# One fused two-layer block: the first FFN's maximum by a TensorE transpose, its second product's bank waits, query tiles between the steps of head 0, and short products before waits

## What is computed

```python
x = x + tanh(g_xattn[0]) * _L0_xattn_ref(ctx, ctx, _layernorm(x), ssm_kernel, D, 8)
x = x + tanh(g_ffn[0])   * _L0_ffn_ref(_layernorm(x), w1, b1, w2, b2)
x = x + tanh(g_xattn[1]) * _L1_xattn_ref(_layernorm(x), ctx, ...)
x = x + tanh(g_ffn[1])   * _L1_ffn_ref(_layernorm(x), ...)
```

```python
def _quant_per_tensor(x):
    scale = jnp.maximum(jnp.max(jnp.abs(x)) / QMAX, EPS)
    q = jnp.clip(jnp.round(x / scale), -QMAX, QMAX).astype(jnp.int8)
    return (q, scale)
h = gelu(_dyn_quant_linear(hidden_state, w1, b1))   # quantises hidden_state
return _dyn_quant_linear(h, w2, b2)                 # quantises h: a second maximum
```

## Time and profile before

| | us |
|---|---|
| median of 3 runs | 646.97 |
| lowest, highest | 645.42, 648.0 |
| profiled execution | 647.98 |
| its span, first to last instruction | 646.1 |
| PE busy | 613.0 |
| DVE busy | 545.4 |
| ACT busy | 484.5 |
| POOL busy | 345.6 |

### The profile page before, as it was taken

The page is one execution under the profiler, slowest core; times in us unless marked ns, Lnnn a source line. Parts: engine busy times, 40 slices in busy tenths (PEclk is TensorE's granted clock), DMA queues, the critical chain, the costliest instruction groups (busy, mean ns, idle before and its releaser), DMA issues.

```text
span 646.1 us, 9452 instructions
## 1 busy us (share of the span) xinstructions
PE 613.0 (95%) x2831; PEld 361.9 (56%) x2861; DVE 545.4 (84%) x1063; ACT 484.5 (75%) x725; POOL 345.6 (53%) x430
## 2 busy tenths in 40 slices
PE   4899999999999899989999999999898999999997
PEld 4677777777777444544445565655433444444443
DVE  2597888889999788985779988889898999999865
ACT  4449786666754898999663567677679999999984
POOL 2479888888873175210001011113488989898861
PEclk9799999999999999999999999999999999999999
DMA  8949997699999364217628940000114666666661
GB/s 305 377 144 287 297 341 252 215 329 340 335 312 312 129 227 162 99 39 285 258 49 161 228 134 16 16 18 0 49 50 132 177 178 177 185 195 163 179 162 49
DMA packets 127860, 118.90 MB, mean 184 GB/s; under 512 B 83456, under 2 KB 90384, under 8 KB 126672
## 3 DMA queue, kind: packets, MB, share of 16 engines
q1 hardware_dynamic: 120384, 104.23, 52.7%
q10 hardware_dynamic: 7440, 14.24, 6.6%
HBM read 68.04 MB, written 30.49 MB: 153 GB/s over the span
## 4 chain that ended last, share of the span: by engine, by line
PE 65%; ACT 11%; DVE 11%; issue 7%; DMA 4%; POOL 1%; SPq 0%; DVEq 0%; ACTq 0%; POOLq 0%
PE ps L1184 22%; PE ps L1473 14%; PE ps L1489 8%; PE ps L1299 5%; ACT turn L970 4%; PE ps L1400 3%; PE ps L1430 3%; ACT arena L917 2%; PE ps L1448 2%; PE ps L1404 2%; PE ps L1193 1%; PE ps L1380 1%; PE ps L1390 1%; DVE turn L1857 1%; DMA arena<-kpad_d 1%
## 5 line engine op out<-in xcount | busy, mean ns | idle before, releaser
L1184 PE MATMUL ps<-arena 128*128 128x288 f32 x640 | 163.5, 413 | 6.2 <-DMA arena<-kpad_d 3.9
L1184 PEld LDWEIGHTS ps<-arena 128*128 128x128 f32 x640 | 121.1, 193 | 39.6 <-issue 4.5
L1473 PE MATMUL ps<-arena 128*128 128x512 bf16 x510 | 113.4, 379 | 3.6 <-DVE arena L2052 3.3
L1473 PEld LDWEIGHTS ps<-arena 128*128 128x128 bf16 x512 | 49.5, 98 | 65.5 <-DVE arena L2052 4.1
L683 POOL TENSOR_TENSOR arena<-arena 128x512 f32<-128x512 f32 x64 | 80.4, 1277 | 9.0 <-DVE arena L2052 8.3
L583 POOL TENSOR_TENSOR arena<-arena 128x1024 f32<-128x1024 f32 x32 | 60.6, 1895 | 22.5 <-issue 11.8
L1489 PE MATMUL ps<-arena 128*128 128x512 bf16 x241 | 57.1, 379 | 2.5 <-ACT arena L1084 0.7
L1299 PE MATMUL ps<-arena 128*128 128x512 bf16 (+1 forms) x248 | 56.2, 379 | 0.9 <-ACT arena L917 0.4
L1340 PE MATMUL ps<-arena 128*128 128x512 bf16 x251 | 55.3, 379 | 1.7 <-DVE arena L1827 1.4
L590 POOL TENSOR_TENSOR turn<-turn 128x512 f32<-128x512 f32 x31 | 40.5, 1308 | 21.6 <-DVE turn L1637 21.6
L2052 DVE SCALAR_TENSOR_TENSOR arena<-ps,up_scale,arena 128x512 f32<-128x512 f32 x64 | 46.6, 744 | 5.9 <-ACT arena L1060 5.0
(11 more groups left out here) (229 smaller groups left out, 1287.6 us busy)
## 6 DMA issues: line engine op xcount, KB each, us to landing
arena<-in_L_ffn_w SPq DMA_DIRECT2D x48, 512.0 KB, 6.0
arena<-kpad_d ACTq DMA_DIRECT2D x16, 512.0 KB, 6.9
hq_d<-arena SPq DMA_DIRECT2D x14, 512.0 KB, 3.1
tern_d<-late SPq DMA_DIRECT2D x24, 256.0 KB, 5.8
arena<-in_ctx SPq DMA_DIRECT2D x4, 1024.0 KB, 12.0
arena<-in_x SPq DMA_DIRECT2D x4, 1024.0 KB, 14.2
arena<-in_L_ffn_w ACTq DMA_DIRECT2D x8, 512.0 KB, 5.6
arena<-in_ctx SPq DMA_DIRECT2D x2, 2048.0 KB, 10.6
```

Source lines behind the costliest of these rows:

```text
L1184: last = pe.matmul(ps[:, 4 * s + lo, 0:NB * PAIRS], toep[:, u, (LB - 1 - lo + li) * P:(LB - lo + li) * P], kv[:, s, li, :], start=(li == 0 ...
L1473: last = pe.matmul(ps[:, bank, :], xq4T[:, s, 4 * j + k, :], w[:, k, c * L:(c + 1) * L], start=(k == 0), stop=(k == LB - 1))
```

## The change

- **Maximum.** PE transposes `am1`, spread over 128 columns, into bank 7 between theta 4 and theta 5; DVE reduces that bank (`amg`). POOL's first `partition_all_reduce` goes; the second stays.
- **Rows in halves.** DVE's two tiles of group 0 are counted on their own; PE turns them first, then ACT's two; DVE copies out in two pieces. All thresholds of `xqb_ready` and `xq_tr` rise by one.
- **Thetas.** On PE thetas 0 to 4 stand before the maximum, 5 before `rows_T(0)`, 6 and 7 behind it. On ACT copy 2 stands before `quant_x(0)`, 3 to 5 between it and `quant_x(1)`, 6 and 7 behind.
- **Fourth weight quarter** is cast by POOL after the second group's norm.
- **Second product.** PE waits for DVE's add out of the bank (`x2_added`). ACT's fourth piece has two tiles, DVE does tiles 14 and 15 after the cast of piece 1; SP's reload of the last x rows waits for that. 22 products of 128x128 before the wait for the weights take the place of ten of 128x512 behind it.
- **Opening.** `toep_load(0, 0)` after two copies; 40 identity transposes; query tiles after blocks 1 and 2; POOL's `pairs(1, 1)` waits for DVE's four normalised tiles.

The diff, cut:

```diff
                     sp.wait_ge(S["hq_ready"], 3)
+                if g == 3:
+                    sp.wait_ge(S["hq_ready"], 6)
...
             norm_x0(1)
+            pool.wait_ge(S["xn0_dve"], 4)
...
             norm_x1(1)
+            pool.wait_ge(S["o_done"], HEADS + 2)
+            pool.wait_ge(S["w1_in"], 16 * 4)
+            w = fw1T[:, :, 3 * L:4 * L]
+            pool.tensor_scalar(w, w.bitcast(I16), 1.0, 0.0, ALU.mult, ALU.add).then_inc(S["w1_ready"], 1)
...
-            pool.wait_ge(S["amax_ready"], 1)
-            pool.partition_all_reduce(amg[:, 0:1], am1[:, 0:1], P, RED.max).then_inc(S["amax_all"], 1)
...
             pool.wait_ge(S["xn1_ready"], NT)
-            pool.wait_ge(S["xqb_ready"], 2)
+            pool.wait_ge(S["xqb_ready"], 3)
...
                 pool.tensor_tensor(x_res[:, t, :], x_res[:, t, :], b2b[:, :], ALU.add).then_inc(S["xb_added"], 1)
-            pool.wait_ge(S["xqb_ready"], NG)
+            pool.wait_ge(S["xqb_ready"], NG + 1)
...
                 pool.tensor_tensor(x_res[:, t, :], x_res[:, t, :], b2b[:, :], ALU.add).then_inc(S["xb_added"], 1)
-            pool.wait_ge(S["xq_tr"], NG)
+            pool.wait_ge(S["xq_tr"], NG + 1)
...
             act.dma_start(kpad_d, kpad[:, :]).then_inc(S["k_stored"], 16)
-            for n in range(G):
+            for n in range(2):
...
             toep_load(0, 0)
-            for n in range(G, 2 * G):
+            for n in range(2, 2 * G):
...
                 normalise_x1(n)
-            for b in range(2, G + 1):
-                theta_out(b)
+            theta_out(2)
...
                 if g >= 2:
-                    act.wait_ge(S["xqb_ready"], g - 1)
+                    act.wait_ge(S["xqb_ready"], g)
...
             quant_x(0)
+            for b in range(3, G + 2):
+                theta_out(b)
             quant_x(1)
-            for b in range(G + 1, NB):
+            for b in range(G + 2, NB):
...
                         act.wait_ge(S["hq_ready"], k + 1)
-                    tiles = 4 if k else 2
+                    tiles = 2 if k in (0, 3) else 4
...
             c_tiles(1, range(G, 2 * G))
-            for n in range(20):
+            for n in range(40):
...
                     pe.wait_ge(S["q_out_act"], G + h - NT // 2 - 1)
-                head(h, h % 2, [late[:, l * P:(l + 1) * P] for l in range(LB)], {2: 0, 3: 1} if h == 0 else None)
+                head(h, h % 2, [late[:, l * P:(l + 1) * P] for l in range(LB)], {1: 0, 2: 1} if h == 0 else None)
...
-            for b in range(NB - 1):
+            for b in range(G + 1):
                 theta(b)
+            pe.wait_ge(S["amax_ready"], 1)
+            pe.transpose(ps[:, 7, 0:P], am1[:, 0:1].to_broadcast([P, P]), identf[:, :]).then_inc(S["amax_all"], 1)
+            theta(G + 1)
...
             def rows_T(g):
-                pe.wait_ge(S["xqb_ready"], g + 1)
...
                 dst = bank_bf(4 + 2 * (g % 2), 2)
-                for n in range(16):
-                    last = pe.transpose(dst[:, n * P:(n + 1) * P], wqb[:, g % 2, n * P:(n + 1) * P], identb[:, :])
-                last.then_inc(S["xq_tr"], 1)
+                parts = (range(16),) if g else (range(8, 16), range(8))
+                for m, part in enumerate(parts):
+                    pe.wait_ge(S["xqb_ready"], g + 2 if g else m + 1)
+                    for n in part:
+                        last = pe.transpose(dst[:, n * P:(n + 1) * P], wqb[:, g % 2, n * P:(n + 1) * P], identb[:, :])
+                    last.then_inc(S["xq_tr"], 1)
...
             rows_T(0)
-            theta(NB - 1)
+            theta(G + 2)
+            theta(G + 3)
...
             last.then_inc(S["swb_made"], 1)
+            for n in range(22):
+                pe.matmul(ps[:, 2, n % 4 * P:(n % 4 + 1) * P], identb[:, :], identb[:, :], start=True, stop=True)
...
-            for n in range(10):
-                pe.matmul(ps[:, 7, :], identb[:, :], fw2T[:, 0, :], start=True, stop=True)
...
                 for j in range(G):
-                    pe.wait_ge(S["x2_done"], G * r + j + 1)
+                    pe.wait_ge(S["x2_added"], G * (r - 1) + j + 1)
...
-            pe.wait_ge(S["x2_done"], NT + 1)
+            pe.wait_ge(S["x2_added"], NT - 3)
...
                     if isinstance(b, int) and b == 0 and k % 2:
-                        pe.wait_ge(S["x2_done"], NT + 3 + k // 2)
+                        pe.wait_ge(S["x2_added"], NT - 1 + k // 2)
...
             v.tensor_copy(b1[:, :], ps[:, 4, 0:FT]).then_inc(S["b1_out"], 1)
-            w1_widen(3)
...
+            v.wait_ge(S["amax_all"], 1)
+            dv.done(v.tensor_reduce(amg[:, 0:1], ps[:, 7, 0:P], AX, ALU.max))
+            dv.wait()
...
             dv.wait()
-            v.tensor_copy(wqb[:, 0, 2 * L:4 * L], wqi[:, 0, 2 * L:4 * L])
+            v.tensor_copy(wqb[:, 0, 2 * L:4 * L], wqi[:, 0, 2 * L:4 * L]).then_inc(S["xqb_ready"], 1)
...
             def rows_out(g):
-                v.wait_ge(S["xq_tr"], g + 1)
-                v.tensor_copy(xqT[:, :, g * L:(g + 1) * L].rearrange("p k (t n) -> p t k n", t=G),
-                              bank_bf(4 + 2 * (g % 2), 2).rearrange("p (t k n) -> p t k n", t=G, k=LB)).then_inc(S["xq_out"], 1)
+                for m, tiles in enumerate((slice(0, G),) if g else (slice(2, G), slice(0, 2))):
+                    v.wait_ge(S["xq_tr"], g + 2 if g else m + 1)
+                    last = v.tensor_copy(xqT[:, :, g * L:(g + 1) * L].rearrange("p k (t n) -> p t k n", t=G)[:, tiles],
+                                         bank_bf(4 + 2 * (g % 2), 2).rearrange("p (t k n) -> p t k n", t=G, k=LB)[:, tiles])
+                last.then_inc(S["xq_out"], 1)
...
                 if g >= 2:
-                    v.wait_ge(S["xq_tr"], g - 1)
+                    v.wait_ge(S["xq_tr"], g)
...
                         v.wait_ge(S["mm2_done"], G * (q - 1))
+                    if (q, c) == (0, 3):
+                        dv.wait()
...
                                   hqi2[:, c % 2, :]).then_inc(S["hq_ready"], 1)
+                    if (q, c) == (0, 1):
+                        v.wait_ge(S["hq_ready"], 4)
+                        dv.done(v.tensor_scalar(hqi2[:, 1, 2 * L:4 * L].rearrange("p (f n) -> p f n", f=2), hid[:, 0, 14:16, :], isx[:, 1:2], None,
+                                                ALU.mult))
...
                     v.wait_ge(S["a_out"], k + 1)
-                    dv.done(v.tensor_tensor(tmp2[:, k % 2, :], ps[:, 2 * j + 1, :], tmp2[:, k % 2, :], ALU.add))
+                    v.tensor_tensor(tmp2[:, k % 2, :], ps[:, 2 * j + 1, :], tmp2[:, k % 2, :], ALU.add).then_inc(S["x2_added"], 1)
...
                         to_residual(k - 1)
-                    dv.wait()
+                    v.wait_ge(S["x2_added"], k + 1)
...
```

8 lines of the change are left out of this document (4 added, 4 removed).

## The result

The changed kernel takes 643.28 us (median of 6 executions, 643.07 to 643.52), the kernel before, beside it, 647.53 (6 executions, 645.42 to 649.51): a ratio of 0.9927, with a 95% interval of 0.9912 to 0.9943. The forecast was 641.3 with a range of 639.5 to 645.0. The profiled execution of the changed kernel took 643.2, with a span of 641.4, 4.7 us shorter than the one of before. Four marks that stand in both traces say where this comes from.

What follows compares the result with a forecast made beforehand. TensorE was taken to carry two thirds of the span, with waits in three stretches: opening 3.9, first FFN 0.85, second FFN 0.95, together 5.7 off 647.98, so 642.3; 1.0 less for the median gives 641.3, range 639.5 to 645.0.

Steps and rivals of the forecast that it cites:

- the gain of load and clock: Opening: head 0's Toeplitz load 1.5 us earlier, clock kept up by 20 added transposes; part of the 3.9 us forecast there.
- step 3: Opening, head 0 on TensorE: 8 passes, put at 2.1 us, behind the second four query tiles in the new order.

Runs made afterwards that it cites:

- the kernel with the all-reduce: First FFN's maximum over partitions again by GpSimd's all-reduce instead of TensorE's transpose, against the changed kernel: 647.12 us, median of 10 executions.

## What to carry to other kernels

When an edit makes the first of several arrivals earlier, look for the one that is second, and for everything that the engine behind it does in order: here the gain of load and clock stopped at a copy that stood behind two instructions of another job, and swapping the two gave 1.2 us, while the early load gave nothing. An idle engine can be filled in two ways, by bringing what it waits for forward or by giving it other work meanwhile, and an edit that moves such work away from the idle time (the tiles ahead of step 3) loses what the others gain. Undo each part alone: of the eight parts undone, one cost 1.0 us, one cost 0.6 and one was worth nothing in the medians, though the change as a whole gained 4.25.

## What the runs showed of the hardware

- One profile can miss what most executions pay: the kernel with the all-reduce took 644.5 where it was profiled, with a clock of 1.000, and 647.1 in the median of the others, whose mean granted clocks are 0.995 to 0.997 in eight cases of nine. The mean also counts what costs nothing: in the profile with 20 transposes the clock is at 0.84 over the last 3.3 us, where TensorE's last product is through.
- TensorE's clock fell after a standstill of 2.12 us behind 20 transposes and stayed after one of 1.95 us behind 40; with 24 transposes in the idle time at the first maximum the mean clock was 0.999 or more in six executions of six, and without them 0.997 or less in eight of ten.
- A pair of elementwise instructions on VectorE took 2.69 us while GpSimd multiplied at the same time, and 1.00 alone; holding GpSimd back for 1.1 us was worth 0.54.
- An all-reduce on GpSimd ran no sooner than 5.6 to 6.4 us after its set-up was asked for, in four kernels; the other engines work meanwhile, and GpSimd itself does nothing else.
